# A graph layer and a top-2 expert layer on one core: VectorE sums a unit between its cast and its subtraction

## The chip, the cores and the metric

One core of one Trainium2 chip. The metric is the device time of one launch, in microseconds (us), as the median of several runs. The kernel before takes 718.91 us (three runs, 718.31 to 721.46).

## What is computed

Input `x` is 128 x 128 x 128 in fp32 (16,384 tokens of width 128). Two residual layers follow each other:

```python
x = x + gnn(layernorm(x), adj, ...)        # two 128x128 products per graph, three sigmoid gates, relu
x = x + ffn(layernorm(x), Wg, bg, W1, b1, W2, b2)

def ffn(x):                                # 8 experts, hidden width 512, top 2 of 8
    top_w, top_i = top_k(xf @ Wg + bg, 2);  top_w = softmax(top_w)
    for e in range(8):
        h = gelu(xf @ W1[e] + b1[e])
        out += w_dense[:, e:e+1] * (h @ W2[e] + b2[e])
```

## The kernel before

**Two stages.** Until about 205 us the first layer, the gates and the routing run in 64 chunks of 1,024 tokens. GpSimd (POOL) writes every routed row into a DRAM table `rows`, ordered by expert (`scatter_rows`, line 646, eight indirect DMAs a chunk). The second stage works on 140 units of 256 rows: 70 units for the first expert of every token, then 70 for the second. Names and numbers k count these units from 0.

**One unit, engine by engine.** SyncE (SP) loads its 256 rows, and weights where the expert changes. TensorE (PE) turns the rows (`unit_turned`, line 1609). ScalarE (ACT) casts them to fp32r (`in_hi`, line 836), and VectorE (DVE) subtracts to get the remainder (`tile_lo`, line 1416). PE multiplies by the first weights, 12 matmuls (`layer1`, lines 1623 to 1625); ACT applies gelu (line 846). DVE casts the result (`hidden_hi`, line 1422) and subtracts again (`hidden_lo`, line 1429, the lower part of the activations); for units below 32 ACT does half of the cast. PE multiplies by the second weights: eight matmuls that need only the cast (lines 1637, 1638), then four that need the lower part (line 1642). ACT adds the bias (`copy_y`, line 858), PE turns the output back (`unit_back`, line 1653), and DVE scales it by the row's weight and adds it to the row (`sum_up`: line 1438 for the address, units from 32 on, and two instructions of line 1443). POOL then sends the unit's rows out with two indirect DMAs (`scatter`, line 691 in the first pass, 688 in the second).

**What sets the order.** Each engine has one order, written out by hand, and semaphores between the engines. In iteration k PE does `layer1(k)`, `unit_back(k-2)`, `layer2(k-1)`, `unit_turned(k+3)`. `unit_turned(k+3)` reuses a PSUM bank and waits until unit k-3 is summed; the second part of `layer2(k-1)` waits for `hidden_lo(k-1)`. DVE does, in iteration k, `sum_up(k-3)`, `tile_lo(k+2)`, `hidden_hi(k)`, `hidden_lo(k)`, and then `between(k)`: pieces of the routing of the last chunks and of the table of units, in iterations 0 to 24.

**POOL's queue.** POOL's order is fixed as well: `scatter` of units 0 to 5, the eight DMAs of `scatter_rows` for chunk 61, units 6 to 9, chunk 62, units 10 to 13, chunk 63, then all other units. `scatter(k)` in the first pass first waits until the rows of unit k-3 have landed and tells SP so (`landed`, line 674).

**SP's queue.** In iteration k SP issues the first-layer weights of unit k+2, its biases, the second-layer weights of k+1 and the rows of k+6 (line 504). The rows of unit k go into the place of unit k-16, and SP waits until those have landed (units 32 to 47 have places of their own and do not wait). At the start of the second pass SP waits for a count of landed units that comes from a table. A wait of SP holds up all that it issues later, weights among it.

Of the kernel before, what the change touches and what calls it, by code (L numbers as in the profile page):

```python
# [53 lines left out]
def wait_turn(eng, sem, each, turn, more):  # L54

    value = turn.group * (each * turn.unroll) + (each * turn.step + more)
    if not isinstance(value, int) or value > 0:
        eng.wait_ge(sem, value)
# [27 lines left out]
def program(nc, x, x_turned, adj, edges, gate_weights, gate_biases, Wg, bg, W1, W2, biases, out):  # L86
# [18 lines left out]
    IN, BACK = 3, 2  # L105
# [19 lines left out]
    def unit(k):  # L125
        return Turn(0, k, ALL, UNITS)
# [14 lines left out]
    with ExitStack() as ctx:  # L141
# [132 lines left out]
        def rows_of_unit(t):  # L274
            return first_rows[t.slot(GR)] if t.index < NE else got[:, t.slot(GR)]
# [46 lines left out]
        def ps_o(t):  # L322
            return bank[:, bank_of_outputs(t.index), 0:TILE].rearrange("p (j m) -> p j m", j=BLK)
# [85 lines left out]
        def _(sp):  # L409
# [75 lines left out]
            def entries(column, first, n, most, least=0, held=table):  # L485
                _, values = nc.values_load_multi_w_load_instructions(
                    held[column:column + 1, bass.ds(first, n)], engines=[mybir.EngineType.SP], min_val=least, max_val=most,
                    skip_runtime_bounds_check_because="VectorE makes the table's entries from counts that lie in these bounds")
                return values
# [384 lines left out]
        def _(dve):  # L874
# [538 lines left out]
            def tile_lo(t):  # L1413
                wait_turn(dve, s_inhi, 1, t, 1)
                k = t.slot(IN)
                dve.tensor_tensor(in_lo[:, k], ps_x(t), in_hi[:, k].bitcast(F32), ALU.subtract).then_inc(s_inlo, 1)  # L1416

            def hidden_hi(t):
                wait_turn(dve, s_mm2, 1, t, -LATE)
                wait_turn(dve, s_act, 2, t, 2)  # L1420
                done = FC // 2 if t.index < NE else 0
                dve.tensor_copy(act_hi[:, t.slot(LATE + 1), done:], act_f[:, t.slot(2), done:]).then_inc(s_hhi, 1)  # L1422

            def hidden_lo(t):
                s = t.slot(LATE + 1)
                wait_turn(dve, s_hhi, 1, t, 1)
                if t.index < NE:
                    wait_turn(dve, s_half, 1, t, 1)
                dve.tensor_tensor(act_lo[:, s], act_f[:, t.slot(2)], act_hi[:, s].bitcast(F32), ALU.subtract).then_inc(s_hlo, 1)  # L1429

            def sum_up(t):
                g, second = t.slot(GR), int(t.index >= NU)
                held = rows_of_unit(t)
                at = TOKEN_AT if second else NEXT_AT

                if t.index >= NE:
                    i = t.index if second else t.index - NE
                    dve.scalar_tensor_tensor(out=to_row[:, g, :], in0=skip[:, i, :], scalar=BIG, in1=got_i[:, g, :, at],
                                             op0=ALU.mult, op1=ALU.max)
                wait_turn(dve, s_o, 1, t, 1)  # L1440
                for j in range(BLK):
                    w = held[:, j, W_AT + second:W_AT + second + 1]
                    last = dve.scalar_tensor_tensor(out=held[:, j, P:2 * P], in0=ps_o(t)[:, j, :], scalar=w,  # L1443
                                                    in1=held[:, j, P:2 * P], op0=ALU.mult, op1=ALU.add)
                last.then_inc(s_done, 1)

            units = range(UNITS)
            for k in units[:IN - 1]:
                tile_lo(unit(k))
            for k in units:  # L1450
                if k - BACK - 1 in units:
                    sum_up(unit(k - BACK - 1))
                if k + IN - 1 in units:
                    tile_lo(unit(k + IN - 1))
                if k == units[-1]:
                    sum_up(unit(k - BACK))
                hidden_hi(unit(k))
                hidden_lo(unit(k))
                between(k)
            for k in units[-BACK:]:  # L1460
# [263 lines left out]
```

## Time and profile before

| | |
|---|---|
| median of the runs | 718.91 us |
| the profiled execution | 719.69 us, span 717.8 us |
| busy, share of the span | PE 91%, DVE 85%, ACT 75%, POOL 70% |
| stage of units, in the profiled execution | 213 to 705 us |
| mean granted clock of PE | 0.96 of full speed |

The page gives busy time by engine; PE is the busiest, but the shares are means over stages. The table of stages, the timelines by engine and the waits, of which the rows below are cut, tell which engine ends a stage last. A row of a timeline gives the start in us, the duration in us, the engine, the line, the operation, what it writes and reads, and, in brackets, the idle time before it and what ended it.

### The profile page before, as it was taken

The page shows a single profiled execution, that of the slowest core. Times are in us where ns is not written, and L with a number is a line of the kernel's source. Part 1 is how long each engine was busy: PE and PEld are TensorE (multiplying, and loading weights), DVE is VectorE, ACT ScalarE, POOL GpSimd, SP SyncE. Part 2 cuts the span into 40 slices and gives each one's busy share as a digit, 9 for nine tenths or more (in the row PEclk, how much of TensorE's full clock was granted, in tenths as well). Part 3 has the DMA queues.
Part 4 walks back from the last instruction along what each step waited for, and adds up shares of the span by engine and source line. Part 5 has one row for each costly group of instructions (what it writes and reads, how often), then busy time and mean ns, then how long its engine had stood idle before and what let it go on. Part 6 is the DMA issues. An engine that isn't in the chain of part 4 may idle for free.

```text
span 717.8 us, 17809 instructions
## 1 busy us (share of the span) xinstructions
PE 654.3 (91%) x4879; PEld 596.8 (83%) x4879; DVE 608.5 (85%) x2041; ACT 541.3 (75%) x1505; POOL 504.2 (70%) x471
## 2 busy tenths in 40 slices
PE   5979898988859999899997999988999999999991
PEld 4646566666539999899997999988999999999991
DVE  5899999999986888987885888885888888888881
ACT  4689999999977978788674767664777776767670
POOL 2553777676764577778887888877777777777774
PEclk9999999999977999999998999998999999999997
DMA  8999995558346897959999975789764444444211
GB/s 293 336 357 279 354 345 180 178 177 309 107 148 182 288 327 254 310 163 300 325 353 319 370 240 159 219 320 354 241 160 128 122 129 120 125 128 125 72 42 33
DMA packets 85497, 161.06 MB, mean 224 GB/s; under 512 B 32631, under 2 KB 36736, under 8 KB 85392
## 3 DMA queue, kind: packets, MB, share of 16 engines
q1 hardware_dynamic: 66032, 112.96, 50.2%
q0 software_dynamic: 18496, 46.70, 17.8%
q8 instruction: 41, 0.67, 0.4%
q14 instruction: 64, 0.52, 0.2%
q10 hardware_dynamic: 864, 0.21, 0.1%
HBM read 104.95 MB, written 57.23 MB: 226 GB/s over the span
## 4 chain that ended last, share of the span: by engine, by line
PE 32%; ACT 23%; POOL 13%; issue 12%; DMA 10%; DVE 8%; SPq 1%; POOLq 0%; DVEq 0%; ACTq 0%
POOL out_dram L688 8%; ACT hs L750 6%; POOL rows L691 5%; ACT row L759 5%; ACT t_loop L741 4%; PE bank L1623 4%; PE bank L1624 4%; PE bank L1625 4%; PE bank L1637 4%; PE bank L1638 4%; PE bank L1642 4%; ACT t_in L734 3%; DMA rows<-row,to_row 3%; PE bank L1609 2%; PE bank L1653 2%
## 5 line engine op out<-in xcount | busy, mean ns | idle before, releaser
L846 ACT ACTIVATE act_f<-bank,b_t 128x256 f32<-128x256 f32 x560 | 220.1, 476 | 22.8 <-PE bank L1625 14.7
L688 POOL DMA_INDIRECT out_dram<-row,to_row x140 | 165.7, 1184 | 57.7 <-issue 56.1
L646 POOL DMA_INDIRECT rows<-row,slot_low x128 | 136.8, 1069 | 62.6 <-issue 34.4
L1429 DVE TENSOR_TENSOR act_lo<-act_f,act_hi 128x1024 fp32r<-128x1024 f32 x140 | 171.9, 1228 | 5.9 <-ACT act_hi L852 0.2
L1422 DVE CAST act_hi<-act_f 128x1024 fp32r<-128x1024 f32 (+1 forms) x140 | 90.5, 647 | 70.1 <-ACT act_f L846 67.7
L836 ACT ACTIVATE in_hi<-bank 128x256 fp32r<-128x256 f32 x140 | 53.9, 385 | 113.4 <-PE bank L1609 113.1
L1623 PE MATMUL bank<-in_hi,w_t 128*128 128x256 f32 x376 | 115.6, 308 | 7.5 <-DMA w_t<-w_split 7.5
L691 POOL DMA_INDIRECT rows<-row,to_row x76 | 94.6, 1245 | 24.7 <-issue 20.9
L1624 PE MATMUL bank<-in_lo,w_t 128*128 128x256 f32 x376 | 107.4, 286 | 0.0
L1625 PE MATMUL bank<-in_hi,w_t 128*128 128x256 f32 x376 | 107.4, 286 | 0.0
L1637 PE MATMUL bank<-act_hi,w_t 128*128 128x256 f32 x376 | 100.9, 302 | 0.1
L1638 PE MATMUL bank<-act_hi,w_t 128*128 128x256 f32 x376 | 92.6, 281 | 0.0
L1623 PEld LDWEIGHTS bank<-in_hi,w_t 128*128 128x128 f32 x376 | 73.1, 194 | 8.0 <-DMA w_t<-w_split 8.0
L1624 PEld LDWEIGHTS bank<-in_lo,w_t 128*128 128x128 f32 x376 | 73.4, 195 | 0.0
L1625 PEld LDWEIGHTS bank<-in_hi,w_t 128*128 128x128 f32 x376 | 73.0, 194 | 0.0
L1637 PEld LDWEIGHTS bank<-act_hi,w_t 128*128 128x128 f32 x376 | 71.3, 190 | 0.5 <-DMA w_t<-w_split 0.3
L1638 PEld LDWEIGHTS bank<-act_hi,w_t 128*128 128x128 f32 x376 | 71.4, 190 | 0.0
L858 ACT ACTIVATE y_t<-bank,b_t 128x256 f32<-128x256 f32 x140 | 65.8, 470 | 3.9 <-PE bank L1642 3.9
L1443 DVE SCALAR_TENSOR_TENSOR row<-bank,row 128x128 f32<-128x128 f32 x216 | 64.7, 339 | 1.3 <-PE bank L1653 1.3
L1642 PE MATMUL bank<-act_lo,w_t 128*128 128x256 f32 x376 | 59.5, 280 | 0.0
L750 ACT ACTIVATE hs<-xs,shift,rstd 128x128 f32<-128x128 f32 x128 | 53.4, 644 | 7.9 <-DVE t_sum L992 5.9
L1416 DVE TENSOR_TENSOR in_lo<-bank,in_hi 128x256 fp32r<-128x256 f32 x140 | 57.6, 412 | 1.5 <-ACT in_hi L836 1.5
(278 smaller groups left out, 1762.2 us busy)
## 6 DMA issues: line engine op xcount, KB each, us to landing
row<-rows SPq DMA_DIRECT2D x108, 260.0 KB, 3.0
w_t<-w_split SPq DMA_DIRECT2D x52, 512.0 KB, 6.3
w_up<-w_split SPq DMA_DIRECT2D x28, 512.0 KB, 6.1
xs<-in_x_dram SPq DMA_DIRECT2D x16, 512.0 KB, 4.7
x_t<-in_x_turned_dram SPq DMA_DIRECT2D x16, 512.0 KB, 6.3
rows<-ends_rep SPq DMA_DIRECT2D x15, 260.0 KB, 7.7
xs<-rows SPq DMA_DIRECT2D x10, 260.0 KB
b_t<-in_biases_dram SPq DMA_DIRECT2D x140, 2.5 KB
```

Source lines behind the costliest of these rows:

```text
L646: pool.indirect_dma_start(out=rows, out_offset=bass.IndirectOffsetOnAxis(ap=slot_low[:, r, b:b + 1], axis=0), in_=row[:, r, b, :], in_offs ...
L688: pool.indirect_dma_start(out=out_rows, out_offset=at, in_=got[:, g, j, P:2 * P], in_offset=None, bounds_check=TOKENS - 1, oob_is_err=Fals ...
L691: pool.indirect_dma_start(out=rows, out_offset=at, in_=rows_of_unit(t)[:, j, :], in_offset=None, bounds_check=NROWS - 1, oob_is_err=False) ...
L750: last = act.activation(hs[:, t.slot(2), b, :], xs[:, t.slot(4), b, :], ACT.Identity, scale=rstd[:, 0, b:b + 1], bias=shift[:, 0, b:b + 1])
L846: last = act.activation(act_f[:, s, c, :], ps_h(t, half)[:, i, :], ACT.Gelu, bias=b_t[:, w, c:c + 1])
L1422: dve.tensor_copy(act_hi[:, t.slot(LATE + 1), done:], act_f[:, t.slot(2), done:]).then_inc(s_hhi, 1)
L1429: dve.tensor_tensor(act_lo[:, s], act_f[:, t.slot(2)], act_hi[:, s].bitcast(F32), ALU.subtract).then_inc(s_hlo, 1)
L1623: pe.matmul(dst, hi, in_hi[:, s], start=True, stop=False)
L1624: pe.matmul(dst, hi, in_lo[:, s], start=False, stop=False)
L1625: last = pe.matmul(dst, lo, in_hi[:, s], start=False, stop=True)
L1637: pe.matmul(ps_y(t), hi, act_hi[:, s, c, :], start=(c == 0), stop=False)
L1638: pe.matmul(ps_y(t), lo, act_hi[:, s, c, :], start=False, stop=False)
```

## The change

In DVE's loop over the units, the sum of a unit is moved. Before, iteration k began with the sum of unit k-3. After, the sum of unit k-2 stands between the cast and the lower part of unit k, behind `tile_lo(k+2)`. The extra sum in the last iteration is no longer needed. Nothing else is edited: the same instructions run, and the last two units are summed behind the loop as before.

```diff
             for k in units:
-                if k - BACK - 1 in units:
-                    sum_up(unit(k - BACK - 1))
                 if k + IN - 1 in units:
                     tile_lo(unit(k + IN - 1))
-                if k == units[-1]:
+                hidden_hi(unit(k))
+                if k - BACK in units:
                     sum_up(unit(k - BACK))
-                hidden_hi(unit(k))
                 hidden_lo(unit(k))
                 between(k)
             for k in units[-BACK:]:
```

## Rows read from the trace of the kernel before

**Rows 1.** The page, part 1: busy us, share of the span, instructions.

```profile
PE 654.3 (91%) x4879; PEld 596.8 (83%) x4879; DVE 608.5 (85%) x2041; ACT 541.3 (75%) x1505; POOL 504.2 (70%) x471
```

**Rows 2.** Stages: us; busy PE, PEld, DVE, ACT, POOL; PE clock, DMA share, GB/s.

```profile
228.70:308.90 80.20, 76.98 (x654) 75.19 (x652) 72.73 (x283) 65.86 (x170) 55.70 (x52) 1.00 0.84 284
...
381.80:387.30 5.50, 5.50 (x29) 5.50 (x29) 1.57 (x2) 1.68 (x4) 3.76 (x5) 0.56 0.99 363
...
492.80:697.50 204.70, 204.70 (x1763) 204.70 (x1761) 178.00 (x377) 146.09 (x377) 151.44 (x127) 1.00 0.48 139
```

**Rows 3.** Timeline of DVE, one unit of the dense part (k = 66).

```profile
455.12 0.69 DVE L1422 CAST act_hi<-act_f 128x1024 fp32r<-128x1024 f32 x1 [0.38 <-ACT act_f L846]
...
455.85 1.23 DVE L1429 TENSOR_TENSOR act_lo<-act_f,act_hi 128x1024 fp32r<-128x1024 f32 x1
...
456.99 0.15 DVE L1438 SCALAR_TENSOR_TENSOR to_row<-skip,row 128x2 int32<-128x2 f32 x1
...
457.06 0.60 DVE L1443 SCALAR_TENSOR_TENSOR row<-bank,row 128x128 f32<-128x128 f32 x2
...
457.58 0.41 DVE L1416 TENSOR_TENSOR in_lo<-bank,in_hi 128x256 fp32r<-128x256 f32 x1
```

**Rows 4.** Timeline of PE, the next unit (k = 67) and the one behind.

```profile
455.64 0.37 PE L1623 MATMUL bank<-in_hi,w_t 128*128 128x256 f32 x1
...
458.28 0.63 PE L1642 MATMUL bank<-act_lo,w_t 128*128 128x256 f32 x4
...
458.89 0.36 PE L1623 MATMUL bank<-in_hi,w_up 128*128 128x256 f32 x1
```

**Rows 5.** Waits of PE, 213 to 310 us: total us, times, longest.

```profile
PE bank L1609 <- DVE w_in L1443: 1.9, 4, 0.5
...
PE bank L1609 <- DVE hs L1443: 0.6, 1, 0.6
PE bank L1609 <- DVE t_loop L1443: 0.5, 1, 0.5
```

**Rows 6.** Timeline of DVE: sum of unit 0, cast of unit 7, sum of unit 5.

```profile
231.66 0.60 DVE L1443 SCALAR_TENSOR_TENSOR w_in<-bank,w_in 128x128 f32<-128x128 f32 x2
...
248.23 0.43 DVE L1422 CAST act_hi<-act_f 128x512 fp32r<-128x512 f32 x1 [0.24 <-ACT act_f L846]
...
250.58 0.60 DVE L1443 SCALAR_TENSOR_TENSOR x_t<-bank,x_t 128x128 f32<-128x128 f32 x2
```

**Rows 7.** Timeline of POOL: first scatters of a run, one dense unit, the end.

```profile
233.07 1.97 POOL L691 DMA_INDIRECT rows<-w_in  x1 [6.93 <-DVE w_in L1443]
...
254.74 0.97 POOL L646 DMA_INDIRECT rows<-row,slot_low  x1 [0.30 <-issue]
...
310.38 0.97 POOL L691 DMA_INDIRECT rows<-t_in  x1 [0.30 <-issue]
...
368.12 1.67 POOL L691 DMA_INDIRECT rows<-row,to_row  x1 [0.30 <-issue]
...
456.25 1.68 POOL L691 DMA_INDIRECT rows<-row,to_row  x1 [0.30 <-issue]
...
705.88 0.97 POOL L688 DMA_INDIRECT out_dram<-row,to_row  x1 [0.30 <-issue]
```

**Rows 8.** Timeline of SP: two issues of unit rows that waited.

```profile
375.81 0.33 SPq L504 DMA_DIRECT2D row<-rows  x1
...
482.13 0.33 SPq L504 DMA_DIRECT2D row<-rows  x1
```

**Rows 9.** Timeline of PE: the two longest waits for weights in the stage of units.

```profile
381.79 0.58 PE L1623 MATMUL bank<-in_hi,w_t 128*128 128x256 f32 x1 [4.08 <-DMA w_t<-w_split]
...
487.07 0.58 PE L1623 MATMUL bank<-in_hi,w_t 128*128 128x256 f32 x1 [3.43 <-DMA w_t<-w_split]
```

**Rows 10.** Timeline of POOL: scatter of unit 136, and the last one.

```profile
700.51 1.24 POOL L688 DMA_INDIRECT out_dram<-row,to_row  x1 [0.53 <-DVE row L1443]
...
709.71 0.97 POOL L688 DMA_INDIRECT out_dram<-row,to_row  x1 [0.30 <-issue]
```

## The prediction

> **What bounds the kernel now.** I read the busy times first: PE 91% [rows 1], a mean over unlike stages. The table of stages comes next [rows 2]: from 492.8 to 697.5 us PE is busy for all of 204.7 us at full clock, 63 units in a row; from 228.7 to 308.9 it is busy for 77.0 of 80.2; from 381.8 to 387.3 its granted clock is 0.56, close to the lower level of 1.2 GHz, behind a pause. Where PE is dense only PE's own work counts: one `layer1` starts at 455.64 and the next at 458.89, so a unit takes 3.25 us [rows 4]. What can be won lies in the pauses, and the waits name two kinds.
>
> First, between 213 and 310 us PE waits for a sum of DVE before it may turn new rows: 1.9 + 0.6 + 0.5 = 3.0 us in six waits [rows 5]. There DVE does a piece of routing in each iteration, and the sum stands behind it.
>
> Second, PE waits 4.08 us at 381.79 and 3.43 us at 487.07 for weights [rows 9]. The timeline of SP says why: it issued no unit rows until 375.81 and 482.13 [rows 8], and the weights stand behind those rows. The first was waiting for the rows of unit 32, the second for the count of landed units. Both come from POOL, which is far behind: it starts on unit 32 at 368.12 [rows 7], while PE is in unit 42. From 254.74 on POOL's gaps are its own 0.30. So the two long pauses end when POOL's queue has come so far, however early PE arrives.
>
> POOL's pace is the thing to read closely. Undisturbed, a scatter takes 0.97 and the next follows after 0.30: a step of 1.27 [rows 7]. The one at 456.25 takes 1.68. Counted back from its end (457.93) by an undisturbed length less about 0.12 of start-up, it was let go at 457.08, and 457.08 is where `hidden_lo` ends (455.85 + 1.23) [rows 3, 7]. The scatter of 233.07 (1.97 long) ends in the same way 0.85 behind the end of a `hidden_lo`. So I read: a scatter that wants to begin while DVE runs `hidden_lo` is held until that ends. Two free steps take 2.54, and 2.54 behind the end of one `hidden_lo`, in a period of 3.25, lies inside the next one (it begins 2.02 behind). So POOL makes two steps a unit and no more: from 310.38 to 368.12 it makes 36 in 57.74 us, 1.60 each, and catches up nothing [rows 7].
>
> **The change part by part.** Sums on 719.69, the profiled execution; that is 0.78 above the median shown, which I take off at the end.
>
> *The work itself.* The same instructions run, but for one order. Before, the cast starts 0.73 ahead of `hidden_lo` though it lasts 0.69, and the address row starts 0.09 before `hidden_lo` ends [rows 3]: the wait for the cast's own semaphore costs about 0.13, and a sum in between covers it. That is 0.1 us of DVE per unit, worth something only where DVE is late, about five units: below 0.5 us, inside the next term.
>
> *Dense units.* `hidden_lo` now stands behind two sums and an address. The sum takes from 456.99 to 457.58, 0.59, and the cast frees the engine 0.09 before its end, so `hidden_lo` starts 0.60 + 0.59 = 1.19 behind the start of the cast instead of 0.73, and ends 2.42 behind it, at 457.54 in this unit instead of 457.08 [rows 3]. PE wants it at 458.28 [rows 4]. The slack of 1.20 falls to 0.74: nothing, 0 us. If that cover were gone, each 0.1 us beyond it would cost 0.1 us in some 110 units. The wait for the turned output is in front of `hidden_lo` now, with `hidden_lo`, `between` and `tile_lo` queued behind it, and PE and ACT behind them; but `unit_back(k-2)` runs right behind `layer1(k)`, before the gelus of which the cast waits, so it is over. `tile_lo` ends at 2.42 - 0.09 + 0.41 = 2.74, inside the 3.25.
>
> *The waits of PE for sums.* The sum now stands one iteration earlier, ahead of `hidden_lo` and the routing: the six waits go, 3.0 us at most. What is late next is `hidden_lo` itself where the routing fills DVE (units 18 to 21). There PE can use only the slack it has, about 1 us, so I take 2.4 us, with 0 and 3.0 as ends.
>
> *POOL's start.* POOL waits for the first sums (6.93 us idle at 233.07), and its unbroken queue begins at 254.74 when unit 5 is out [rows 7]. The sum of unit 5 moves from 250.58 to behind the cast of unit 7, 248.23 + 0.34 = 248.6 [rows 6], 2.0 earlier; the wait of PE that the sum of unit 0 (231.66) ended, 0.6 by the gap, is gone ahead of that. So the queue begins 2.6 us earlier.
>
> *What POOL loses on the way.* From 254.74 to 310.38 it makes 40 steps in 55.64 us; free they would take 50.8, so it is held for 4.8 [rows 7]. How long one unit holds it follows from the length of the unit: what is left over behind whole steps of 1.27. At 3.25 that is 0.7, at 3.9 (units with the wait for a sum) 3 steps fit and 0.1 is left. The change makes three or four of these units short, at 0.6 each, and with PE ahead one more unit falls into the stretch: I take 2.1 more. Bounds: nothing held at all, 4.8 less; held as in the dense part, (57.74 - 36 x 1.27)/36 = 0.33 a step, 13.4 in all, 8.6 more. I take the low middle because four units stay near 3.8 with DVE as their bound. So POOL reaches unit 32 earlier by 2.6 - 2.1 = 0.5 us (ends: 7.4 earlier, 6.0 later).
>
> *The long pauses.* The first one ends 0.5 earlier; PE comes to it 2.4 earlier, so it grows by 1.9. In it DVE stands still and POOL steps at 1.27 instead of 1.63: it wins 1.9 x (1 - 1.27/1.63) = 0.4, which the second pause gives back to the end. Together 0.9 us. Of PE's 2.4 the rest is lost in the pauses.
>
> *The end.* At the end POOL is behind too: the last eight scatters, from 700.51 to 709.71, follow at nearly its own step [rows 10]. Unit 136 now is summed 0.67 instead of 1.94 behind a cast [rows 3], 1.3 earlier; two of the scatters fall into a later `hidden_lo` and lose 0.3 each, one that a cast held by 0.27 is free. Gain 0.9 (ends 0 and 1.3).
>
> Sum: 0.9 + 0.9 = 1.8 us; 719.69 - 1.8 = 717.9 in the profiled execution, 717.1 as a median.
>
> The Trainium skill, "SBUF — State Buffer", section "Who interferes with whom", agrees with one half of the reading above: a VectorE instruction with two SBUF inputs and a GpSimd instruction that reads SBUF share a port. It also says, as an inference, that a `tensor_tensor` does not hold up the making of a DMA's descriptors, and only the faster copies and casts do. The trace speaks against this half: the hold ends with the subtraction. Should it be right all the same, POOL would lose nothing more on the way; that is rival C.
>
> **The rivals.** Half a per cent, 3.6 us, is about what a measurement of this kernel can tell from no change.
>
> A. The held time does not grow, since the units of the routing stay long or fall well. Then POOL keeps its 2.6, the longer pause adds nothing, and 2.6 + 0.9 gives 3.5; with luck in the holds two or three more. For it: 40 steps against 15 units is a small number, and what is left over jumps between 0 and 1.2. Against it: shorter units hold POOL more. Time 715.2.
>
> B. Slower. The units of the routing, freed of PE's waits, come down to the dense period, and POOL is locked to two steps a unit from 254.74 on instead of from about 315. Then it loses 8.6, not 2.1: 6.0 late at unit 32. PE, 2.4 early, meets a first pause that is longer by 8.4, in which POOL wins back 8.4 x 0.22 = 1.8. With the end's 0.9 the total is 3.3 later: 722.2. It decides from a held time of about 9 us between the first scatter of chunk 61 and unit 14 (now 4.8). For it: the lock is plain in the dense part. Against it: DVE needs about 3.8 us for each of units 18 to 21 whatever the order.
>
> C. The hold comes from casts alone. The rows of POOL and DVE in step say no. POOL keeps its 2.6, as in A, and the time is 715.4.
>
> D. The lower part comes too late for PE in the dense part after all, because something else in the cast or the sum grows, by 0.84 against a slack of 0.74. At 0.1 us in 110 units: 728. The rows leave too much slack for that.
>
> E. It does not do what it says: the waits of PE go to `hidden_lo` one for one, POOL waits as before, and only the end is won or not: 718.9.
>
> **Chances.** Forecast 0.50 (its own range 714.5 to 719.5), A 0.20, B 0.15, C 0.04, D 0.04, E 0.07. Below 715.3 lie about half of A and C and a tenth of the forecast, together with a little for a luckier A: 0.22. Above 722.5 lie half of B and D: 0.12. Between them 0.66. The range goes from 713.2 (A with luck) to 722.0 (most of B).
>
> **What would show it.** Right: no wait of `unit_turned` for a sum between 213 and 310; in a dense unit `hidden_lo` starting about 1.2 behind its cast, and PE at 3.25 a unit with no idle time ahead of line 1642; the first `scatter_rows` row of chunk 61 near 252.1; POOL at two steps a unit in the dense part, its long scatters ending 0.85 behind the end of `hidden_lo`; SP's two late issues less than 1.5 us from 375.8 and 482.1; the last scatter about 0.9 earlier, counted from PE's last matmul. Wrong: idle time of PE ahead of line 1642 in dense units (D); the two pauses for weights gone or shorter by several us (A), or longer by more than 4 (B); POOL stepping at 1.27 through `hidden_lo` (C).

## The result, and the profile after

After the change the kernel takes 722.54 us (median of 17 runs, 719.41 to 725.48); before, beside it, 720.79 (17 runs, 716.42 to 722.50). The ratio is 1.0032, with a 95% interval of 1.0016 to 1.0048: slower by 0.3%, some 2.3 us by the ratio (the two medians lie 1.75 apart). The forecast was 717.1, 1.8 us faster, with a range up to 722.0. The error is larger than the interval, and on the other side. The profiled execution has a span of 719.1 against 717.8. Of the experiments below, e4 and e10 had one slow execution each (799.1 and 1606.05 us), and their figures are those of the other five.

The page, busy time by engine, and the stages that answer to [rows 2]:

```profile
PE 654.0 (91%) x4879; PEld 595.7 (83%) x4879; DVE 594.4 (83%) x2041; ACT 540.0 (75%) x1505; POOL 509.6 (71%) x471
```

```profile
229.30:310.10 80.80, 79.78 (x682) 78.58 (x680) 71.91 (x289) 67.94 (x175) 57.98 (x52) 1.00 0.84 281
...
386.59:391.31 4.72, 4.72 (x29) 4.72 (x29) 0.82 (x3) 1.68 (x4) 3.50 (x5) 0.66 0.97 313
493.50:698.20 204.70, 204.70 (x1763) 204.70 (x1761) 172.38 (x376) 145.68 (x377) 156.43 (x126) 1.00 0.50 139
```

In the first stage PE now stands idle for 1.0 us (80.80 less 79.78), before for 3.2. The dense stage is 204.70 long as before. DVE is busy 14 us less on the page and POOL 5 us more (before 608.5 and 504.2); a scatter that is held counts as busy, so POOL's 5 us are the first sign of what went wrong.

One dense unit, DVE and then PE, as in [rows 3, 4]:

```profile
457.17 0.69 DVE L1422 CAST act_hi<-act_f 128x1024 fp32r<-128x1024 f32 x1 [0.51 <-ACT act_f L846]
...
457.85 0.61 DVE L1443 SCALAR_TENSOR_TENSOR row<-bank,row 128x128 f32<-128x128 f32 x2
458.37 1.22 DVE L1429 TENSOR_TENSOR act_lo<-act_f,act_hi 128x1024 fp32r<-128x1024 f32 x1
```

```profile
457.68 0.37 PE L1621 MATMUL bank<-in_hi,w_t 128*128 128x256 f32 x1
...
460.33 0.63 PE L1640 MATMUL bank<-act_lo,w_t 128*128 128x256 f32 x4
460.94 0.36 PE L1621 MATMUL bank<-in_hi,w_up 128*128 128x256 f32 x1
```

The subtraction starts 1.20 behind the cast and ends at 459.59; PE takes it up at 460.33, and a unit is still 3.26 long. (PE's line numbers are two lower than before.)

PE's waits from 213 to 310 us (total, times, longest), in the place of [rows 5]: no wait for a sum is left, and three short ones for `act_lo` (units 20 to 22) have come.

```profile
PE bank L1607 <- DMA w_in<-rows: 1.6, 2, 1.1
PE bank L1651 <- ACT y_t L858: 1.3, 1, 1.3
PE bank L1640 <- DVE act_lo L1429: 0.9, 3, 0.4
```

POOL's timeline answers to [rows 7, 10]:

```profile
251.51 1.18 POOL L691 DMA_INDIRECT rows<-x_t  x1 [0.30 <-issue]
253.00 1.35 POOL L646 DMA_INDIRECT rows<-row,slot_low  x1 [0.30 <-issue]
...
311.17 1.29 POOL L691 DMA_INDIRECT rows<-t_in  x1 [0.30 <-issue]
...
366.50 1.42 POOL L691 DMA_INDIRECT rows<-row,to_row  x1 [0.30 <-issue]
...
457.47 1.23 POOL L691 DMA_INDIRECT rows<-row,to_row  x1 [0.30 <-issue]
459.01 1.42 POOL L691 DMA_INDIRECT rows<-row,to_row  x1 [0.30 <-issue]
...
701.49 1.05 POOL L688 DMA_INDIRECT out_dram<-row,to_row  x1 [0.30 <-issue]
...
710.94 0.97 POOL L688 DMA_INDIRECT out_dram<-row,to_row  x1 [0.30 <-issue]
```

In the dense part both scatters of a unit are held now. The one at 457.47 ends 0.85 behind the end of the cast (457.86), the one at 459.01 ends 0.85 behind the end of the subtraction (459.59); 1.23 + 1.42 and twice 0.30 make 3.25. Before, one of the two was held for longer, and the other not at all. From 253.00 to 311.17 there are 40 steps, 58.17 us; before it was 55.64. (The first layer has 16 chunks of 1,024 tokens, 128 scatters of line 646 at eight a chunk, and not 64: the last three, called 61 to 63 above and in the expectations, are chunks 13 to 15.)

SP's two late issues and PE's waits for weights behind them, as in [rows 8, 9]:

```profile
374.75 0.33 SPq L504 DMA_DIRECT2D row<-rows  x1
...
482.81 0.33 SPq L504 DMA_DIRECT2D row<-rows  x1
```

```profile
386.59 0.58 PE L1621 MATMUL bank<-in_hi,w_t 128*128 128x256 f32 x1 [2.78 <-DMA w_t<-w_split]
...
488.67 0.52 PE L1621 MATMUL bank<-in_hi,w_t 128*128 128x256 f32 x1 [3.73 <-DMA w_t<-w_split]
```

**One table for all that follows.** Unit 0 starts anywhere between 212.5 and 216.0 in the traces of all kernels, with the same code ahead of it; so I count from the start of `layer1` of unit 3. A loss is the time between two such starts less 3.257 us a unit (the mean dense unit): before, units 3 to 25 take 312.14 - 228.67 = 83.47, less 22 x 3.257, which is 11.8. "Held" is POOL's time from the first scatter of chunk 13 to the first of unit 14, less 40 x 1.275 (the prediction's 4.8 takes 1.27 a step). The tail is counted from the start of unit 139 to the start of the last scatter. The second to last column is the whole way from unit 3 to the last scatter. Names are those of the experiments below; "cut" marks those in which the subtraction is cut into pieces.

| kernel | loss 3-25 | 25-43 | 43-77 | 77-139 | tail | unit 3 to last scatter | held |
|---|---|---|---|---|---|---|---|
| before | 11.8 | 0.0 | 14.5 | -0.4 | 12.2 | 481.0 | 4.6 |
| after | 9.1 | 3.0 | 14.3 | -0.4 | 12.7 | 481.7 | 7.2 |
| after, run again | 9.1 | 6.4 | 11.7 | 0.8 | 12.7 | 483.7 | 10.0 |
| e1 | 9.5 | 1.5 | 12.2 | -0.3 | 12.4 | 478.3 | 4.9 |
| e2 | 11.8 | 0.0 | 14.8 | -0.1 | 12.7 | 482.1 | 4.6 |
| e3 | 9.1 | 7.0 | 10.5 | 1.2 | 12.2 | 482.9 | 10.0 |
| e9 | 9.2 | 2.1 | 12.8 | 0.4 | 13.4 | 481.0 | 4.3 |
| e4, cut | 11.0 | 1.7 | 4.2 | 0.1 | 11.4 | 471.4 | 7.8 |
| e5, cut | 13.0 | 1.5 | 3.2 | 0.4 | 12.6 | 473.7 | 2.3 |
| e6, cut | 10.9 | 0.6 | 5.7 | 0.2 | 12.6 | 472.9 | 3.0 |
| e7, cut | 11.0 | 0.6 | 6.2 | 0.1 | 12.6 | 473.5 | 3.0 |
| e10, cut | 9.9 | 1.1 | 4.5 | 0.1 | 12.4 | 471.0 | 2.1 |

PE gains its 2.7 us up to unit 25, and from unit 25 to 77 it loses 17.3 where before it lost 14.5. The tail is 0.5 longer. Together: -2.7 + 2.8 + 0.5 = 0.6 in this trace, and 2.6 in that of the run again; the 2.3 of the ratio lies between. Each row is one execution.

### The profile page after: what moved, and what is told of

Its sections match the earlier page's. It is cut to its first block and busy times, and to the rows that moved or that the text cites. A ratio compares the mean times of both kernels' runs of the same rounds, so it can differ in the third digit from the quotient of the medians.

```text
span 719.1 us, 17809 instructions
## 1 busy us (share of the span) xinstructions
PE 654.0 (91%) x4879; PEld 595.7 (83%) x4879; DVE 594.4 (83%) x2041; ACT 540.0 (75%) x1505; POOL 509.6 (71%) x471
## 5 line engine op out<-in xcount | busy, mean ns | idle before, releaser
L688 POOL DMA_INDIRECT out_dram<-row,to_row x140 | 171.3, 1224 | 53.0 <-issue 51.6
```

The lines of the kernel that those rows point to most:

```text
L688: pool.indirect_dma_start(out=out_rows, out_offset=at, in_=got[:, g, j, P:2 * P], in_offset=None, bounds_check=TOKENS - 1, oob_is_err=Fals ...
```

## The experiments

Each one was timed in turn with the kernel before on one chip; ratios are to that kernel, with 95% intervals.

**e1_behind_lower: the sum as early, but behind the subtraction.**

```diff
                 hidden_hi(unit(k))
+                hidden_lo(unit(k))
                 if k - BACK in units:
                     sum_up(unit(k - BACK))
-                hidden_lo(unit(k))
                 between(k)
```

> The sum of unit k-2 stands behind hidden_lo(k) and ahead of the routing piece. In dense units this is the order of before (cast, hidden_lo, sum); in the units with routing the sum is early, as after. Theory P (POOL's queue ends the two long pauses; what slows the changed kernel is that POOL is held by DVE more often): PE's waits for sums go, POOL's queue begins 1.5 to 2.5 us earlier, and in the dense part POOL is held once per unit (about 0.7) and in the second pass idles 0.2 per unit, so the end is as before: 719.5 to 721.5, 1 to 2.5 us under the changed kernel. Rival W (PE is hurt because it arrives early at rows and weights: more pauses between units 27 and 54, a cold clock more): as slow as the changed kernel, 722 to 723.

Measured: 717.50 us, ratio 0.9961 (0.9943 to 0.9980). The early sum alone brings the gain that was forecast for the change, and more; PE's units are as short as after the change (loss 9.5 against 9.1). POOL is held for 4.9 instead of 7.2. So short units alone do not hold POOL; what the two orders differ in is the sum standing between the cast and the subtraction. POOL of e1, the first scatter of chunk 13 and the first of unit 14:

```profile
253.07 0.97 POOL L646 DMA_INDIRECT rows<-row,slot_low  x1 [0.30 <-issue]
...
308.96 0.97 POOL L691 DMA_INDIRECT rows<-t_in  x1 [0.30 <-issue]
```

**e2_dense_only and e3_routing_only: each half of the change alone.** e2 keeps the old order up to unit 25 and uses the new one from there; e3 the reverse.

```diff
             for k in units:
+                if k - BACK - 1 in units and k <= 25:
+                    sum_up(unit(k - BACK - 1))
...
                 hidden_hi(unit(k))
-                if k - BACK in units:
+                if k >= 25:
                     sum_up(unit(k - BACK))
```

```diff
             for k in units:
+                if k > 25:
+                    sum_up(unit(k - BACK - 1))
...
+                if k == units[-1]:
+                    sum_up(unit(k - BACK))
                 hidden_hi(unit(k))
-                if k - BACK in units:
+                if k - BACK in units and k < 25:
                     sum_up(unit(k - BACK))
```

> Order of before for units below 25, order of after from unit 25 on. Theory P: up to unit 25 nothing differs from before; in the dense part POOL is held twice per unit (by the cast and by hidden_lo) and has no idle time left in the second pass, so a delay of one scatter is not made good and the last scatter lies 0.5 to 1.5 us later against PE's last matmul: 721 to 722.5. Rival W: no early PE, so no extra pauses; the sums come earlier in dense units and the end gains 0.9: 719 to 720.5.

> Order of after for units below 25, order of before from unit 25 on. Theory P: PE 2 to 3 us ahead at unit 25, POOL not ahead at unit 14, so pauses for weights grow by what PE was ahead; end as before: 720 to 721.5. Rival W: as slow as the changed kernel or slower, 722 to 723.5, with the extra pauses between units 27 and 54 as there.

Measured: e2 721.07, ratio 1.0014 (0.9998 to 1.0031); e3 721.08, ratio 1.0022 (1.0000 to 1.0044). Neither alone is sure to be slower, but together they make 1.0036, what the change costs. In e3 POOL takes 60.96 us from the first scatter of chunk 13 to the first of unit 14, in e1 55.89, 5.1 less, and PE of e3 then waits for a step that SP's queue has not reached. POOL of e3, and the waits of PE from 305 to 372 us, of e3 and of the change run again:

```profile
253.07 1.35 POOL L646 DMA_INDIRECT rows<-row,slot_low  x1 [0.30 <-issue]
...
314.03 1.34 POOL L691 DMA_INDIRECT rows<-t_in  x1 [0.30 <-issue]
```

```profile
PE bank L1625 <- SPq L525: 4.0, 2, 2.3
```

```profile
PE bank L1621 <- SPq L525: 2.8, 2, 2.6
```

In e2 the tail is as long as after the change (12.7), in e3 as before (12.2): the loss at the end belongs to the new order in the dense part. Two scatters of e2 there, both held:

```profile
601.32 1.18 POOL L688 DMA_INDIRECT out_dram<-row,to_row  x1 [0.54 <-issue]
602.80 1.22 POOL L688 DMA_INDIRECT out_dram<-row,to_row  x1 [0.30 <-issue]
```

**e4_split4: the change, with the subtraction in four.** The same elements, in four instructions of 128x256.

```diff
-  dve.tensor_tensor(act_lo[:, s], act_f[:, t.slot(2)], act_hi[:, s]..., ALU.subtract).then_inc(s_hlo, 1)
+  for c in range(FC):
+      last = dve.tensor_tensor(act_lo[:, s, c], act_f[:, t.slot(2), c], act_hi[:, s, c]..., ALU.subtract)
+  last.then_inc(s_hlo, 1)
```

> The changed kernel with hidden_lo as four subtractions of 128x256 instead of one of 128x1024; the same result. Theory P: POOL gets its turn between two of the pieces, so no hold is longer than about 0.35 us; its step in the dense part falls from 1.63 to 1.3 to 1.45, it catches up, and the pauses for weights near units 44 and 74 shrink by several us: 709 to 717. Rival W: DVE has 0.2 us more work per unit and the pauses stay: 722 to 723.5. A third case, that POOL gets no turn between pieces that follow each other at once: the holds stay, 722 to 723.

Measured: 707.46, ratio 0.9843 (0.9814 to 0.9871), some 14 us less than the change by the ratios, though DVE works longer (four pieces take 1.42 instead of 1.22). In the dense part POOL gets in between the pieces; where the four start at 343.12, POOL's next steps are 1.27, 1.37 and 1.28 (the last to 346.97):

```profile
343.05 0.97 POOL L691 DMA_INDIRECT rows<-xs  x1 [0.30 <-issue]
344.32 1.06 POOL L691 DMA_INDIRECT rows<-hs  x1 [0.30 <-issue]
345.69 0.97 POOL L691 DMA_INDIRECT rows<-hs  x1 [0.30 <-issue]
```

```profile
343.12 1.42 DVE L1430 TENSOR_TENSOR act_lo<-act_f,act_hi 128x256 fp32r<-128x256 f32 x4
```

The losses of units 43 to 77, some 14 us before and after, fall to 4.2. POOL's first scatter of unit 32 stands 133.14 behind the start of unit 3, before 139.45. This shows that POOL's queue ends the long pauses, and that the hold by the subtraction makes it late. A part of the gain is PE's clock: before, units 45 and 75, behind the two pauses, had a mean granted clock of 0.56 and 0.53 and took 5.47 and 5.71 us, 4.7 more than two dense ones; in e4 the granted clock is 1.00 from 220 to 690 us.

Not all of it went as expected. POOL does not always get in: in the stretch with routing the scatter of 302.02 took 2.21 and was let go only at the end of the fourth piece (301.97 + 1.42), one of 299.03 took 2.68, and the held time up to unit 14 was 7.8, no less than after the change. What the cut wins comes behind that. Up to unit 25, where DVE is late, it costs: 11.0 for 9.1, and in e5 13.0 for 11.8.

**e5_before_split4: the same split in the kernel before.** The diff is that of e4, on the order of before.

> The kernel before with hidden_lo as four subtractions of 128x256; the same result. Theory P (POOL's queue ends the long pauses, and holds by hidden_lo slow POOL): holds of 0.7 go, POOL's step in the dense part falls to 1.3 to 1.4, the pauses near units 44 and 74 shrink to about 3 us together; PE's waits for sums (3 us) now reach the end, so it is up to 3 us slower than the changed kernel with the same split: 708.5 to 712.5. Rival (the split helps only where the sum stands between cast and subtraction, since it parts the two places that hold POOL): 717 to 721.

Measured: 711.94, ratio 0.9884 (0.9851 to 0.9917). Most of e4's gain is the split's. But with the holds short the change is worth some 3 us by the ratios (e4 against e5; their intervals overlap a little, and e6, e7 and e10, with the early sum too, lie at 0.983 to 0.985). In the traces e4 is 2.0 shorter than e5 up to unit 25 and 1.2 in the tail: what the prediction saw in the early sum is there once POOL doesn't take it back.

**e6_behind_split4: the order of e1 with the split of e4.**

> The sum behind hidden_lo and ahead of the routing, and hidden_lo as four subtractions. Theory P: PE's waits for sums are gone and POOL is hardly held: 705.5 to 709, the fastest so far. Rival (the gain of the early sum is lost in the pauses whatever POOL does): 709 to 712, no better than the split of the kernel before.

Measured: 708.58 (707.25 to 710.69), ratio 0.9831 (0.9799 to 0.9863): no different from e4, and both beat the kernel before and the change. Once the subtraction is in pieces it no longer matters on which side of it the sum stands. The page of e6:

```profile
PE 649.8 (92%) x4879; PEld 590.3 (83%) x4879; DVE 636.7 (90%) x2461; ACT 539.7 (76%) x1505; POOL 493.3 (70%) x471
```

DVE is busy for 42 us more than after the change and the kernel is 14 us faster; POOL is "busy" for 16 us less with the same instructions.

**e7_behind_split4_cast2: e6, and the cast in two.**

```diff
-  dve.tensor_copy(act_hi[:, t.slot(LATE + 1), done:], act_f[:, t.slot(2), done:]).then_inc(s_hhi, 1)
+  for c in range(done, FC, FC // 2):
+      last = dve.tensor_copy(act_hi[:, t.slot(LATE + 1), c:c + FC // 2], act_f[:, t.slot(2), c:c + FC // 2])
+  last.then_inc(s_hhi, 1)
```

> As the one before, with the cast too in two halves of 128x512 (units from 32 on). Theory P: holds by the cast fall from up to 0.6 to up to 0.3, POOL ahead by a little in the dense part of the first pass, where the pauses are short already, and 0 to 0.7 us at the end: 705 to 708.5. Against it: DVE gets 0.06 us more per unit, without effect as long as it idles 0.3.

Measured: 709.16, ratio 0.9833 (0.9802 to 0.9864). Nothing more is won: the holds that the cast still makes do not set the time.

**e8_after_again: the change once more,** unedited, on the chip of e5 to e7.

> The changed kernel once more, for a second profile of it on the chip of these runs. Theory P: POOL's held time between the first scatter of chunk 61 and unit 14 is again 7 to 10 us, against 4.6 to 4.9 where hidden_lo follows the cast at once; time 721.5 to 723.5. If the held time is near 5 and the time still over 721, the holds of the routing units are not what slows it.

Measured: 722.06, ratio 1.0023 (1.0000 to 1.0045), which agrees with the first 1.0032. Its trace shows how much the held time hangs on where POOL happens to stand: 10.0 instead of 7.2. In it, as in e3, one scatter begins together with a subtraction, is held through it and through two copies of the routing right behind (`ends_rep`, line 1336), ends 0.85 behind the second copy and is 1.51 longer than a free one; in the first trace of the change a scatter meets only the end of the first copy and is 0.06 longer.

**e9_tile_between: another instruction in the gap.** e1, but with `tile_lo(k+2)`, 0.4 us long, between the cast and the subtraction.

```diff
             for k in units:
+                hidden_hi(unit(k))
                 if k + IN - 1 in units:
                     tile_lo(unit(k + IN - 1))
-                hidden_hi(unit(k))
+                hidden_lo(unit(k))
                 if k - BACK in units:
                     sum_up(unit(k - BACK))
-                hidden_lo(unit(k))
```

> As the run with the sum behind hidden_lo, but with tile_lo(k+2) moved between the cast and hidden_lo: the two stand apart by 0.4 us, and no sum is between them. Theory G (what costs is the gap: a scatter that the cast lets go has its next start 1.27 later, just behind a hidden_lo that follows at once, and inside one that starts 0.4 to 0.5 later): held time between chunk 61 and unit 14 at 7 to 10 us, two holds per unit in the dense part, 720.5 to 723. Rival S (what costs is the sum itself in that place, for instance by the PSUM bank or the unit's rows it touches): held time near 5, as with the sum behind, 716 to 718.5.

Measured: 719.85, ratio 1.0012 (0.9988 to 1.0036). Against e1 it loses 0.5%. In the dense part it does what the sum in the gap does, two held scatters a unit (1.24 and 1.16), and its tail is the longest, 13.4:

```profile
601.01 1.24 POOL L688 DMA_INDIRECT out_dram<-row,to_row  x1 [0.54 <-issue]
602.56 1.16 POOL L688 DMA_INDIRECT out_dram<-row,to_row  x1 [0.30 <-issue]
```

In the routing it does not: POOL is held for 4.3, less than in e1. There 11 scatters end 0.85 behind a subtraction, 3.5 us in all; after the change it is 15 with 6.7 us, in e1 8 with 3.9. So a gap makes more holds, but how long they are depends on what stands in it; that was not settled.

**e10_behind_split2: e1, with the subtraction in two** instructions of 128x512.

```diff
+  for c in range(0, FC, 2):
+      last = dve.tensor_tensor(act_lo[:, s, c:c + 2], act_f[:, t.slot(2), c:c + 2], act_hi[:, s, c:c + 2]..., ALU.subtract)
```

> The sum behind hidden_lo, and hidden_lo as two subtractions of 128x512 (0.64 each) instead of four pieces. Theory P says that POOL is locked to two steps a unit only where one hold can exceed 0.7 (period 3.25 less two free steps of 1.27): with pieces of 0.64 it is not locked, its step in the dense part is 1.3 to 1.5 and the time within 2 us of the four pieces: 707.5 to 711. If the two pieces act as one, 716 to 718.5.

Measured: 708.77, ratio 0.9848 (0.9813 to 0.9883), no different from four pieces. A pair takes 1.29:

```profile
343.17 1.29 DVE L1430 TENSOR_TENSOR act_lo<-act_f,act_hi 128x512 fp32r<-128x512 f32 x2
```

Two free steps of POOL take 2.54 of a unit's 3.25 and leave 0.7; a hold by a piece of 0.64 fits into that, one by 1.23 does not. By this reckoning the size of a piece is enough; no size between 0.64 and 1.23 was run.

## Why the prediction was wrong

Counted from unit 3 to the last scatter, the forecast was 1.8 less, and the trace has 0.6 more (2.6 in the run again). Of this error of 2.4 (4.4), 1.4 lies at the end in both traces and 1.0 (3.0) ahead of it.

**What held.** *The work itself:* DVE's idle time ahead of the cast grew from 0.38 [rows 3] to 0.51, the 0.1 a unit. *Dense units:* 1.19 was forecast between cast and subtraction, 1.20 came, PE lost nothing. *The waits of PE for sums:* 2.4 forecast, 2.7 gained, and `hidden_lo` of units 20 to 22 is what is late next. *POOL's start:* counted from unit 3, its queue begins 253.00 - 229.26 = 23.7 behind, before 26.1: 2.3 earlier, 2.6 was forecast.

**The step that failed first: "What POOL loses on the way".** I took 2.1 us more, because three or four units become short. It was 2.5 and, in the run again, 5.4, and the cause was another, as e1 shows with units as short: that 2.1 is near 2.5 is luck. The prediction had weighed the new place of the subtraction for PE, and for POOL only in two scatters at the end. What it does to POOL can be read from DVE and POOL side by side. Before, DVE and then POOL:

```profile
255.99 0.42 DVE L1422 CAST act_hi<-act_f 128x512 fp32r<-128x512 f32 x1
256.44 1.23 DVE L1429 TENSOR_TENSOR act_lo<-act_f,act_hi 128x1024 fp32r<-128x1024 f32 x1
```

```profile
256.02 1.24 POOL L646 DMA_INDIRECT rows<-row,slot_low  x1 [0.30 <-issue]
257.56 0.97 POOL L646 DMA_INDIRECT rows<-row,slot_low  x1 [0.30 <-issue]
```

The first scatter is let go as the cast ends at 256.41, and that is also the moment at which the subtraction begins. The scatter runs beside it, and when the next one begins at 257.56, the subtraction (to 257.67) is all but over: 0.97. Cast and subtraction, back to back, cost POOL one hold of 0.27. After the change, DVE:

```profile
251.42 0.43 DVE L1422 CAST act_hi<-act_f 128x512 fp32r<-128x512 f32 x1 [0.16 <-ACT act_f L846]
251.76 0.61 DVE L1443 SCALAR_TENSOR_TENSOR xs<-bank,xs 128x128 f32<-128x128 f32 x2
252.28 1.22 DVE L1429 TENSOR_TENSOR act_lo<-act_f,act_hi 128x1024 fp32r<-128x1024 f32 x1
```

POOL's two scatters beside it are the first two of its timeline above. The one of 251.51 is again let go by the cast (251.51 + 1.18 - 0.85 = 251.84). The sum stands in between, so the subtraction comes half a microsecond later and is still running when the next scatter begins at 253.00; this one is let go where it ends, at 253.50 (252.28 + 1.22), 0.38 longer than a free one. Over the stretch 15 scatters are held by a subtraction, 6.7 us, before 7 with 3.7. Why the same in e9, with `tile_lo` in the gap, gives many but short holds stays open, so the mechanism is shown for the dense part and for the sum's place, not for every instruction that could stand there.

**"The long pauses" failed next, in place and in size.** I had PE keep its 2.4 us up to the first long pause and lose 1.5 of them in the two. It lost them earlier, in units 27 (4.77 long), 29 (4.18) and 34 (3.80). Units 29 and 34 are as long in e1 (4.25 and 3.77); unit 27 is what the change adds. Before, PE loses nothing between units 25 and 43; there POOL reaches unit 14 1.8 us ahead of PE's start of unit 25. After the change it is 1.1 behind it, and the loss 3.0; in the run again 4.0 behind and 6.4; in e3 4.0 and 7.0; in e1 0.2 ahead and 1.5. SP's rows of units 30 and 31 take the places of units 14 and 15 (`t_in` and `t_loop` in the rows) and wait for those to land, and weights and biases stand behind them in SP's queue. SP's waits from 300 to 350 us after the change, and PE's first matmul of unit 28:

```profile
SPq L504 <- DMA rows<-t_in: 8.4, 1, 8.4
...
SPq L504 <- DMA rows<-t_loop: 2.2, 1, 2.2
```

```profile
321.34 0.39 PE L1621 MATMUL bank<-in_hi,w_t 128*128 128x256 f32 x1 [1.27 <-SPq L525]
```

Before, the same two waits of SP are 8.6 and 1.7 long, but PE comes later and does not meet them. No run took this wait away by itself, and it is not all: in e5, e6, e7 and e10 POOL is 3.2 to 4.6 ahead there and 0.6 to 1.5 are lost all the same; why is open. The prediction had named that wait in the description of SP and never asked when it would begin to bind. While PE and DVE stood there, POOL stepped freely (six scatters of 0.97 in a row from 319.28), and it came to unit 32 2.2 earlier, counted from unit 3, where 0.5 was forecast (366.50 - 229.26 = 137.24, before 139.45). PE won nothing by it: what comes after is nearly the old sum (14.3 for 14.5), with losses in units 52 and 53 (3.86 and 3.84) that were not there before, so all of PE's gain was given back by unit 77.

**"The end" failed too.** 0.9 was to be gained, 0.5 is lost: 12.7 from the start of unit 139 to the last scatter, before 12.2. The early sum is there, but POOL is not in time to use it. POOL's second pass before, and after, at the same event: the second scatter of unit 112, at 625.20 and at 624.64, begins 0.14 behind the end of the sum of unit 113, although its own unit was summed long before. No sum is late there; the same scatter has a pause of 1.15 to 1.63 ahead of it in every trace here, and why is open.

```profile
625.20 0.97 POOL L688 DMA_INDIRECT out_dram<-row,to_row  x1 [1.15 <-DVE row L1443]
626.47 1.06 POOL L688 DMA_INDIRECT out_dram<-row,to_row  x1 [0.30 <-issue]
627.83 0.97 POOL L688 DMA_INDIRECT out_dram<-row,to_row  x1 [0.30 <-issue]
629.34 1.22 POOL L688 DMA_INDIRECT out_dram<-row,to_row  x1 [0.53 <-issue]
```

```profile
624.64 1.84 POOL L688 DMA_INDIRECT out_dram<-row,to_row  x1 [1.42 <-DVE row L1443]
626.78 1.23 POOL L688 DMA_INDIRECT out_dram<-row,to_row  x1 [0.31 <-issue]
628.31 1.42 POOL L688 DMA_INDIRECT out_dram<-row,to_row  x1 [0.30 <-issue]
```

Before, three short scatters make up the delay and by 629.34 POOL waits for sums again (0.53). After, every pair is held to 1.23 + 1.42 + 0.60 = 3.25, the length of a unit: no idle time is left, and a delay of 1.5 us stays to the end. Up to there POOL was 1.3 earlier against PE than before (11.3 behind the start of its unit instead of 12.6), which is the 1.3 that I had worked out.

**The rivals.** B's time, 722.2, and its point (a held time of 9; it was 7.2 and 10.0) came nearest. But it reasoned from short units as well, which e1 takes away, put the loss into the first long pause and had the end gain 0.9, so its number is in part luck. A's held time, about that of before, came with the order of e1 (4.9 for 4.6); its own sum of 3.5 gives 715.4, not 715.2. C is not it, though casts hold scatters too (62 of the 140 in the second pass, by about 0.25 each, after the change). For D and E nothing speaks.

The Trainium skill, "SBUF — State Buffer", section "Who interferes with whom", says that where VectorE and GpSimd meet at the shared port, whoever issues first keeps it for the whole instruction and the other one blocks. The rows agree for the subtraction ahead of the scatter (let go at its end, 253.50). The other way a scatter holds for a moment only. Where the two begin within 0.05 us of each other, either can be the one held: six times before the change the scatter took 0.97 and the subtraction 1.27 to 1.30 instead of 1.22, as here, POOL and then DVE:

```profile
260.11 0.97 POOL L646 DMA_INDIRECT rows<-row,slot_low  x1 [0.30 <-issue]
```

```profile
260.10 1.27 DVE L1429 TENSOR_TENSOR act_lo<-act_f,act_hi 128x1024 fp32r<-128x1024 f32 x1
```

Once it runs, a scatter is not held again: after the change 14 that had run for 0.15 us or more when a subtraction began took 0.97. Against the inference of the Trainium skill that a `tensor_tensor` leaves the making of descriptors alone the rows decide less than the prediction said: the scatter also reads its row numbers (`slot_low`, `to_row`), and only its beginning is held. What the hold costs is shown: cutting that one instruction in two took 1.1% off, some 8 us (e10 against e1 by their ratios).

## What to carry to other kernels

When an instruction is moved on one engine, look also at the engines that it holds, and lay the timelines over each other at the new place. A queue that is late by a fixed step a unit, with no slack, turns any single delay into time at the end; look for what holds its steps before winning time for another engine. A long instruction that holds another engine can be cut into pieces, here shorter than the free time of that engine's period; the busiest engine may then get busier and the kernel faster.

## What the runs showed of the hardware

- A scatter that begins while a subtraction of 1.22 us runs is held until that ends. In the other direction little is seen: the subtraction at 256.36, with a scatter running since 255.93, took 1.22 too and the scatter 0.97, and where both begin within 0.05 us the subtraction was at most 0.08 longer (1.30 at 240.91, before). Where the scatter is the one held there, it takes some 2.0 (2.04 at 465.27, after the change), so the held time hangs on hundredths of a us.
- Two pieces of 0.64 were as good as four of 0.35: ratios 0.9848 and 0.9831 (e10 and e6).
- One scatter of e3 and of the change run again was held through a subtraction and the copies behind it, 1.51 longer than a free one; in the first trace of the change the copies held one by 0.06. So the held time of one program was 7.2 in one execution and 10.0 in another.
- Behind PE's pause of 2.78 us that ended at 386.59 the mean granted clock was 0.66, between the levels of 1.2 and 2.4 GHz, and that unit took 4.72 us instead of 3.25: such a pause costs more than its length, before [rows 2] and after the change. In e4, where these pauses are nearly gone, the granted clock stayed at 1.00 from 220 to 690 us.
